# Attention heads stage: dividing six PSUM banks 4 + 2 instead of 3 + 3

## What is computed

```python
xn = _layernorm(x, ln_gamma, ln_beta)
q = proj(Wq) / math.sqrt(DH); k = proj(Wk); v = proj(Wv)   # 16 heads of 16
scores = einsum('bhid,bhjd->bhij', q, k)
scores = scores + rel[:, clip(i - j, 0, 128)]
scores = where(i >= j, scores, -inf)
y = softmax(scores) @ v
return x0 + y @ Wo.T
```

## Time and profile before

| | |
|---|---|
| median of 3 runs | 2445.11 us |
| the profiled execution | 2448.93 us |
| its span, first to last instruction | 2447.2 us |
| mean granted TensorE clock | 0.93 |
| heads stage, first fill to last matmul and sum | 1589 to 2363 us |
| busy over the whole span: PE, DVE, ACT, POOL | 85%, 61%, 39%, 13% |

### The profile page before, as it was taken

The page is one execution under the profiler, slowest core; times in us unless marked ns, Lnnn a source line. Parts: engine busy times, 40 slices in busy tenths (PEclk is TensorE's granted clock), DMA queues, the critical chain, the costliest instruction groups (busy, mean ns, idle before and its releaser), DMA issues.

```text
span 2447.2 us, 38521 instructions
## 1 busy us (share of the span) xinstructions
PE 2071.2 (85%) x12810; PEld 1560.6 (64%) x12810; DVE 1486.5 (61%) x4394; ACT 955.9 (39%) x1944; POOL 308.4 (13%) x300
## 2 busy tenths in 40 slices
PE   4599999976999965999999736478998998999966
PEld 3488888865788944888888625324554455545445
DVE  7754444357455577543434588577776686687548
ACT  4223333322333342233232234325555555655643
POOL 4320000032000043200000242311001101100000
PEclk8799999988999987999999858769999999999988
DMA  8111011011000031201010130433242242333002
GB/s 266 63 61 31 28 30 29 27 50 39 1 1 1 1 108 63 67 28 32 27 32 25 45 90 16 80 51 60 41 53 54 54 53 49 58 43 39 3 9 69
DMA packets 84044, 114.84 MB, mean 47 GB/s; under 512 B 12216, under 2 KB 73824, under 8 KB 80736
## 3 DMA queue, kind: packets, MB, share of 16 engines
q1 hardware_dynamic: 77424, 94.80, 17.8%
q0 software_dynamic: 6432, 17.57, 2.2%
HBM read 69.17 MB, written 43.17 MB: 46 GB/s over the span
## 4 chain that ended last, share of the span: by engine, by line
PE 60%; DVE 26%; issue 4%; ACT 4%; POOL 3%; DMA 2%; SPq 0%; DVEq 0%; ACTq 0%; POOLq 0%
PE psum L811 10%; PE psum L809 10%; PE psum L810 10%; PE psum L126 5%; PE psum L2337 4%; PE psum L128 4%; PE psum L127 4%; DVE mt L2225 4%; PE psum L2316 3%; PE psum L898 3%; DVE m L2213 3%; PE psum L2296 2%; DVE stats L160 2%; DVE m L2222 2%; PE psum L2320 2%
## 5 line engine op out<-in xcount | busy, mean ns | idle before, releaser
L2176 ACT ACTIVATE pt<-psum 128x512 f32<-128x512 f32 (+3 forms) x768 | 333.7, 493 | 275.0 <-DVE psum L2251 180.2
L774 DVE SCALAR_TENSOR_TENSOR h<-psum,xg,sg 128x128 f32<-128x128 f32 x592 | 166.9, 344 | 408.8 <-PE psum L898 404.5
L586 ACT ACTIVATE sg<-psum 128x512 f32<-128x512 f32 x180 | 107.5, 597 | 531.5 <-PE psum L811 531.5
L809 PE MATMUL psum<-w_hi,xt_hi 128*128 (+1 forms) x720 | 288.3, 400 | 5.9 <-DVE xt_lo L739 5.3
L810 PE MATMUL psum<-w_lo,xt_hi 128*128 (+1 forms) x720 | 285.9, 397 | 0.0
L811 PE MATMUL psum<-w_hi,xt_lo 128*128 (+1 forms) x720 | 285.5, 397 | 0.0
L2296 PE MATMUL psum<-ks,qs 96*128 96x512 bf16 (+3 forms) x768 | 235.8, 347 | 44.9 <-DMA ks<-qk_scr 21.9
L2316 PE MATMUL psum<-qs,ks 99*128 99x512 bf16 (+3 forms) x768 | 239.4, 335 | 24.8 <-ACT pt L2176 19.1
L809 PE MATMUL psum<-w_hi,ht_hi 128*128 (+1 forms) x720 | 219.3, 305 | 8.3 <-DVE x L789 8.3
L2225 DVE CUSTOM_DVE_ANT_0 mt<-psum,band_q 128x256 bf16<-128x256 f32 (+1 forms) x512 | 204.7, 400 | 17.8 <-PE psum L2296 7.3
L2320 PE MATMUL psum<-band,ident_r 128*128 128x256 f32 (+1 forms) x864 | 215.1, 338 | 0.0
(11 more groups left out here) (285 smaller groups left out, 4252.8 us busy)
## 6 DMA issues: line engine op xcount, KB each, us to landing
xg<-w_dram SPq DMA_DIRECT2D x54, 256.0 KB, 3.2
qk_scr<-parts SPq DMA_DIRECT2D x32, 384.0 KB, 2.5
qs<-qk_scr SPq DMA_DIRECT2D x96, 128.0 KB, 7.1
ks<-qk_scr SPq DMA_DIRECT2D x96, 128.0 KB, 7.7
xg<-rows_in SPq DMA_DIRECT2D x74, 132.0 KB, 2.2
rows_out<-yb SPq DMA_DIRECT2D x74, 128.0 KB, 1.7
x<-x_dram SPq DMA_DIRECT2D x4, 1024.0 KB, 8.7
out_dram<-x SPq DMA_DIRECT2D x4, 1024.0 KB, 4.5
```

Source lines behind the costliest of these rows:

```text
L774: ins = dve.scalar_tensor_tensor(out=h[i % 2][:, e, :], in0=u[:, e, :], scalar=xg[j % XSLOT][:, at:at + 1], in1=sg[i % 2][:, e, :], op0=AL ...
L809: pe.matmul(out, a[0], b[0], start=first, stop=False)
L2176: act.activation(pt[n % NPT][:, 0:q1 - q0], st_bank(n)[:, 0:q1 - q0], ACT.Exp).then_inc(*exped.up())
```

## The change

The score banks become four, and the ring keeps two. `st_bank` gives bank 2 + n % 4, so that the scores use banks 2 to 5; the ring uses 6 and 7. The wait before score n is for the exponential of score n - 4, and every use of the ring waits for the use two back. No instruction, order or other buffer is changed. (`exped(k)` waits for the first k exponentials.)

```diff
             MX = (*ahead.USES, "max_far", "max", "max_turn", "y_turn", "yt_turn", "wo")
-            mx_ring = Ring([u for u in order if u[0] in MX], [psum[:, 5 + i, :] for i in range(3)])
+            mx_ring = Ring([u for u in order if u[0] in MX], [psum[:, 6 + i, :] for i in range(2)])
             y_banks = [psum[:, c, :] for c in range(CB)]
             NPT = 3 * HG
+            NSC = 4
...
-                st_bank = lambda n: psum[:, 2 + n % 3, :]
+                st_bank = lambda n: psum[:, 2 + n % NSC, :]
...
-                            if n >= 3:
-                                pe.wait_ge(*exped(n - 2))
+                            if n >= NSC:
+                                pe.wait_ge(*exped(n - NSC + 1))
```

## The result

The changed kernel takes 2540.04 us (median of 5 runs, 2537.15 to 2543.04) against 2445.11 before: 1.0382 times as long [1.0367, 1.0397]. The forecast was 2527, the range 2468 to 2565. The profiled execution is itself the one of 2540.04 us (span 2538.3), 91.1 above the profiled one of before, where the sum had said 82. In the kernel after, lines behind 2069 stand one further down: L2297 is the fill that was L2296, L2317 the score, L2177 the exponential, L2338 the value.

A forecast was written before the change was run, and what follows sets the result against it. The ring's depth was taken to decide, with PE and DVE bounding the heads stage in turn. From the profiled 2448.93 us, + 90 (ring) - 8 (tail) = +82 gave 2531, or 2527 us on the median's scale; range 2468 to 2565.

The forecast's parts named there:

- main term: Heads stage, 1625 to 2297 us: two ring banks instead of three cost 111 ns on each of 832 uses, taken as 90 us.
- hand layouts: Two stretches retimed with release two back: 2.9 us per 30 fills (97 ns each); with projection 2.0 us late, 135 ns per use.
- share of the groups with projection: Projection steps stand beside 6 of 16 head groups, so 6/16 of the ring uses were priced at 135 ns, the rest at 97.
- Why it doesn't catch up: Values or projections keep PE from the ring 0.4 to 1.5 us; three filled banks cover this, two leave DVE dry.
- Part 1, in the middle: Fourth score bank between 1622 and 2297 us: worth 0, since the ring holds PE back first; other end 29 us.
- almost vanish: Sign in the profile after: PE's waits before the score line until an exponential nearly disappear, in the tail too.
- The tail: After 2297 us, ring almost unused: the fourth score bank gains 8 us, from 0 to 20 cells x 0.53 = 11.
- The start: Stage's first 33 us, only fills on PE: a fill fits beside the reduction before it, so 0 to 1 us lost.
- DVE's busy time: Sign in the heads stage: DVE's busy time stays and its idle time grows by as much as the stage.
- Rival 1: Score waits bound, third ring bank only lead: up to 37 us faster, 2408 us, if ring costs under 44 ns per use; 0.05.
- Rival 2: Late fills delay DVE only singly, no lateness carried on: 50 ns per use, 2450 to 2479 us; chance 0.15.
- Rival 3: PE stops more, its granted clock falls: at 0.94 throughout at most 42 us more, 2569; sign below 0.97 from 1720; chance 0.10.

The follow-up runs named there:

- e1: The changed kernel with three score banks instead of four, so two ring banks and one bank empty; 2553.93 us, 1.0452 times the kernel before.
- e5: The kernel before with value matmuls cut from up to 512 columns to 32 in all cells but each sum's first; 2422.83 us (0.9909).
- e6: The changed kernel with value matmuls cut to 32 columns in all cells but each sum's first; 2511.07 us (1.0270).
- e10: The changed kernel with the query blocks in the order 7, 3, 6, 2, 5, 1, 4, 0; 2532.59 us (1.0350).
- e8: The kernel before with short value matmuls (as e5) and also without PE's bias pairs; 2442.34 us (0.9980).
- e9: The changed kernel with short value matmuls (as e6) and also without PE's bias pairs; 2560.75 us (1.0471).
- e7: The kernel before up to the last maximum; after it the scores have four banks and the ring two; 2441.28 us (0.9982).
- e4: On the changed kernel: three score banks, two ring banks for the maxima's fills alone, one for all other ring uses; 2525.73 us (1.0324).
- e3: Three ring banks as in the kernel before, but two score banks and one bank empty; 2495.46 us (1.0207).

## Why the prediction was right, and where it was not

**Forecast and main term.** 90 us were laid out for the ring from 1625 to 2297, and the middle grew by 95.4 (114 ns per use; taken: 111). The ring's third bank is the cause, by a run that changes it alone: e1 is 108 us slower by the medians, and in the profiles its start, middle and tail are 6.1, 99.2 and 0.7 longer. Both hand layouts held to within 0.05 us at the places read above; the first one was 0.5 us short at its end. The first stretch cost 112 ns per use and a plain group 4.7 us or 92; the layout's 97 lies between, so some of that agreement is luck.

What was mis-sized is the share of the groups with projection. The term gave them 6/16 of 832 uses at 135 ns, 42 us, and the six (0, 1, 4, 5, 8, 9) grew by 54.8; it gave the rest 50, and groups 2, 3, 6, 7 and 10 to 13 grew by 38.1, what is left of the middle by 2.5. By the list of the order the six hold 395 of the 834 uses and not 6/16, since the projection's own steps, the output steps of groups 4 and 8 and the first groups' additional fills are in them. So they cost 139 ns per use (112 to 168 from group to group), near the 135 laid out, and the eight others, with 418 uses, 91. The 139 has more in it than the ring, though: all of the lower clock that after has more than before (below) stands in these six groups.

**Why it doesn't catch up.** This step failed as put. Not the values mainly (30% of a plain group's price, e5 and e6), nor one place in the order (e10). What the rows show in their place is the turn itself: release, 0.06 us, fill, 0.36 to 0.43 us to DVE's start, reduction, release. The reading argued from them: with two banks every fill that PE reaches late, behind a score, a bias pair or a value, leaves DVE no second filled bank; DVE's lateness then delays PE's next fill. That PE's scores are the other 70% was only argued: e8 and e9 could not show it, and their groups 6 and 10 lean the other way, to the round trip by itself. The stage's start shows what it can cost: PE has nothing but fills there, and two banks cost 6.0 us over 49 uses, some 120 ns each, but at a clock of 0.50. How the 70% divide at full clock stays open.

**Part 1, in the middle.** The term 0 was too small: three score banks instead of four cost 0.9 us per plain group (42.8 against 41.9). Of the 14 us between the medians of e1 and after 5 are in the tail, which leaves 9 for the rest; the profiled middles differ by 3.8. So some 4 to 9 us are gained along the middle, between the ends 0 and 29. Groups 1 and 5, with projection and like half-rate time in both kernels, gain nothing. By a count of starts on PE that come later than the step before them explains (an estimate, since the ordinary distance of two starts has to be chosen), the stops at score banks in the middle fell from some 20 us to 2, as foretold, and those at ring banks rose from some 55 to 150. The loader's row before L2317 doesn't show this: 53.4 us until an exponential remain of 90.4, since the loader is idle also while PE is streaming. The sign "almost vanish" was set on the wrong row.

**The tail.** -4.5 us instead of -8. The wait in the cell of the earlier trace rows did go, 0.52 us. The term was too large, since the cells after the first don't all lose 0.53: in the count above the tail's score stops fell by some 7 us, and PE got part of that back as other waits. e7, with a clock of 1.00 in its tail, gains 6.2 where after, with 0.97, gains 4.5; how much of the 1.7 is the clock's is not shown. e1 to after is 5.2.

**The start.** +6.0 instead of 0 to 1. All five kernels with the fills on two banks and the same order have it (after, e1, e4, e6, e9: 40.5 to 40.7), and those with three or four have not (34.5 to 34.9), so it is the ring's. The step that failed took the fill's 0.42 us from a stretch at full clock. Here the clock is 0.50: the fill of 1605.14 us gets DVE started 0.65 us later, and with the 0.06 before it that is longer than any one reduction (the longest is the 0.69 of this row).

```profile
1605.14 0.94 PE L2297 MATMUL psum<-ks,qs 96*128 96x512 bf16 x2 [0.58 <-DVE m L2226]
1605.79 0.69 DVE L2214 TENSOR_REDUCE m<-psum 128x1 f32<-128x512 f32 x1 [0.26 <-PE psum L2297]
```

**DVE's busy time** was to stay and grew by 19.1 us in the stage, with the same instructions at the same durations (415 and 687 ns). Records of instructions that follow without a wait overlap: the reduction of 2331.20 ends at 2331.76 and the next starts at 2331.67. Each break in DVE's row of work removes such an overlap from the account: the durations of DVE's instructions in the stage add up to 671 us in both profiles, and 122.7 us of overlap became 104.0. Idle time grew by 97 - 19 = 78 us and not by as much as the stage.

**The rivals.** Rival 1 (score waits are the bound) is out: its point was 44 ns per ring use, and the ring cost 92 to 114. In its own terms it was a question of which of two like gaps is the bound; e1 to e3 had to give each bank a price. The rule named there, the Trainium skill's (Perfetto Trace Analysis, Optimization Strategy), that a gap that keeps repeating can mean too little PSUM, would ask for a bank at both. Rival 2 (no carry, 50 ns) is out by the same figures. Rival 3 (the clock) is partly true. Its sign was a granted clock below 0.97 between 1720 and the stage's end, and from 1700 to 2394 it is 0.98. But from 1626 to 1700 it is 0.78, where before it was 0.92 in the 74 us from 1622:

```profile
1622.00:1696.00 74.00, 62.69 (x370) 33.79 (x371) 53.70 (x186) 41.48 (x87) 14.61 (x11) 0.92 0.22 43
```

The middle's half-rate time rose from 13 to 68 us (37.5 in e1), all of the rise in the six groups with projection. What that costs can be estimated from groups that differ in it between after and e1. Group 8 in after:

```profile
2062.60:2135.60 73.00, 61.06 (x340) 32.95 (x337) 42.93 (x146) 33.51 (x70) 8.63 (x8) 0.91 0.22 37
```

The same group in e1:

```profile
2068.30:2138.60 70.30, 57.49 (x339) 31.55 (x335) 42.88 (x146) 33.34 (x70) 8.60 (x8) 0.98 0.22 39
```

After is 2.6 us longer with 10.3 us more at half rate. Groups 0 and 9 are 2.4 and 1.4 longer in after with 19.4 and 3.4 more, group 4 is 2.5 longer in e1 with 3.5 more there. That is 0.1 to 0.7 us per us at half rate, by whether the fourth score bank is credited with the 0.9 of a plain group or, as in groups 1 and 5, with nothing. By the least of these the 54 us more of after cost some 7 of the 95 us; 27 is the most that half the clock can cost in 54 us (an estimate, not isolated). The Trainium skill (TensorE: Matmul & The Clock Gate, A second HAM failure mode: psum-queue depth-cycling) tells of short stops at PSUM banks that make the clock swing. Here the trace agrees in part: with more stops the lower level shows more often, beside projections (13 to 68 us), while in the plain groups, which have their stops too, the clock stays at 1.00.

**How the sum came out near.** In part by luck. The misses partly cancel: start +6.0 (no term of the sum), middle +5.4, tail +3.5, rest of the execution -5.8, together 9 of the 13 us by which the forecast on the median's scale is low; the other 4 are the scale itself, whose 3.8 us between profiled run and median were not there after. The middle is itself two misses: by the profiles a ring of two costs 99.2 us and not 90 (101 by the medians), and the score bank's gain of 3.8 (9 by the medians) was left out. In the readings, PE's busy share goes up to 95% between 2100 and 2200 us and ACT's to 57%, where the prediction has 94 and 56; nothing hangs on it.

## What to carry to other kernels

Give each bank a price by the step that it holds up: lay out some 30 uses by hand with the release two or three back, carry the lateness on, and do it at the clock of that stretch; the size of a wait in a row doesn't choose between two sides that both wait. Between the two engines that take turns here, the step from two banks to three was worth 108 us and the step to four 6, the latter beside two score banks that held PE back themselves. Count the uses of each kind of stretch from the order and not by the number of groups. With fixed banks, look for a stretch in which one side is unused and lend its bank there, as in e7.

## What the runs showed that was not expected

Leaving work out of PE went with a slower kernel: without bias pairs e8 is 20 us above e5, at a granted clock of 0.78 over the stage against 0.93. An experiment that takes work away must be read with its clock beside it. And DVE's busy time depends on how its instructions follow one another, by about 0.09 us for each break (2331.76 against 2331.67 above), with the same instructions.
